# First attention: the first scores of two units copied by one ScalarE instruction across two PSUM banks

## The reference, cut to what matters

```python
q, k, q2, k2, v = (proj(Wq), proj(Wk), proj(Wq2), proj(Wk2), proj(Wv))
q, k, q2, k2 = (_apply_rotary(a, cos, sin) for a in (q, k, q2, k2))
scores = jnp.einsum('bqhd,bkhd->bhqk', q, k)
scores2 = jnp.einsum('bqhd,bkhd->bhqk', q2, k2)
pattern = scores / Dh * (scores2 / Dh)
pattern = jnp.where(causal[None, None, :, :], pattern, 0.0)
z = jnp.einsum('bhqk,bkhd->bhqd', pattern, v)
```

## Time and profile before

| | |
|---|---|
| median of three runs | 1599.43 us |
| lowest and highest | 1596.18 and 1599.50 us |
| the profiled execution, its own time | 1599.61 us |
| its span, first to last instruction | 1597.8 us |
| first attention within the span | about 27 to 575 us |
| copies of first scores, L376 | 384, mean 596 ns |
| products, L443 | 384, mean 686 ns |
| masks, L319 | 256, mean 1273 ns |
| PE busy, share of the span | 75% |
| mean granted TensorE clock | 0.838 of full speed |

### The profile page before, as it was taken

One profiled execution on the slowest core, in us unless ns is written; L12 is line 12 of the kernel. 1 busy time (PEld: TensorE's weight loads), 2 busy tenths in 40 slices (PEclk: granted clock), 3 DMA queues, 4 the chain that ended last, 5 costly groups with the idle time before them and its releaser, 6 DMA issues. The chain is left out here.

```text
span 1597.8 us, 34549 instructions
## 1 busy us (share of the span) xinstructions
PE 1191.3 (75%) x11004; PEld 800.7 (50%) x11004; DVE 972.9 (61%) x2744; ACT 696.4 (44%) x1450; POOL 773.6 (48%) x744
## 2 busy tenths in 40 slices
PE   1899999999999967477887904549996548878880
PEld 0344444444444446256666703449996426656660
DVE  4566666767666654888874043925555488878302
ACT  0666667676766624322222405545552612222240
POOL 0577777777777720045556720035550014446661
PEclk9999999999999965577887956869996557888795
DMA  5000000000000022012112140000003101111217
GB/s 141 1 1 0 0 0 0 0 0 0 0 0 0 1 60 77 3 27 60 50 43 55 53 118 11 0 10 0 0 0 86 50 14 39 45 42 50 56 52 217
DMA packets 67972, 54.50 MB, mean 34 GB/s; under 512 B 12865, under 2 KB 57281, under 8 KB 67905
## 3 DMA queue, kind: packets, MB, share of 16 engines
q1 hardware_dynamic: 51392, 32.70, 7.5%
q0 software_dynamic: 8192, 16.79, 3.7%
q10 hardware_dynamic: 8320, 4.19, 0.9%
HBM read 32.69 MB, written 20.97 MB: 34 GB/s over the span
## 5 line engine op out<-in xcount | busy, mean ns | idle before, releaser
L319 POOL TENSOR_TENSOR patt_aa<-patt_aa,causal_aa 128x512 f32<-128x512 f32 x256 | 319.1, 1273 | 100.8 <-DVE patt_aa L443 100.8
L443 DVE TENSOR_TENSOR patt_aa<-p_second_aa,first_aa 128x512 f32<-128x512 f32 x384 | 247.5, 686 | 163.1 <-ACT first_aa L376 161.3
L1231 POOL DMA_INDIRECT rows_e<-norm_rows,index_e x128 | 123.6, 966 | 369.5 <-DVE index_e L955 329.5
L376 ACT ACTIVATE first_aa<-p_first_aa 128x512 f32<-128x512 f32 x384 | 208.4, 596 | 146.8 <-PE p_first_aa L534 143.0
L534 PE MATMUL p_first_aa<-q_t_aa,k_t_aa 32*128 32x512 f32 x768 | 217.4, 642 | 30.4 <-ACT first_aa L376 30.4
L534 PE MATMUL p_second_aa<-q_t_aa,k_t_aa 32*128 32x512 f32 x768 | 233.3, 642 | 0.0
L1143 PE MATMUL p_cnt_e<-reach_e,ones_e 128*128 128x240 bf16 x448 | 89.8, 337 | 102.9 <-DVE reach_e L1001 102.8
L1246 POOL DMA_INDIRECT ffn_rows<-yb_e,index_e x128 | 130.6, 1020 | 58.1 <-issue 32.3
L1077 PE MATMUL p_h_e<-rows_t_e,w_e 128*128 128x512 f32 x256 | 148.6, 710 | 0.2
L553 PEld LDWEIGHTS p_z_aa<-patt_aa,v_aa 128*32 128x32 f32 x3072 | 74.9, 109 | 123.9 <-issue 68.2
L1194 ACT ACTIVATE hid_e<-p_h_e,b_e 128x512 f32<-128x512 f32 x128 | 87.9, 688 | 102.6 <-PE p_h_e L1077 102.4
(11 more groups left out here) (229 smaller groups left out, 2278.6 us busy)
## 6 DMA issues: line engine op xcount, KB each, us to landing
norm_rows<-norm_n SPq DMA_DIRECT2D x32, 256.0 KB, 2.3
w_e<-L_ffn_w SPq DMA_DIRECT2D x32, 256.0 KB, 2.8
buf_r<-ffn_rows SPq DMA_DIRECT2D x16, 512.0 KB, 5.7
out<-x ACTq DMA_DIRECT2D x8, 512.0 KB, 8.2
rows_e<-norm_rows,index_e POOLq DMA_INDIRECT x128
ffn_rows<-yb_e,index_e POOLq DMA_INDIRECT x128, 2.3
b_e<-L_ffn_b SPq DMA_DIRECT2D x16, 64.0 KB, 3.7
lanes<-c_lanes SPq DMA_DIRECT2D x1, 256.0 KB, 3.0
```

The source lines that it names most:

```text
L319: pool.tensor_tensor(patt[n % LAG][:, b, :, :], patt[n % LAG][:, b, :, :], causal[:, None, :].broadcast_to([P, 4, P]), ALU.mult).then_inc( ...
L376: act.activation(first[n % 2][:, b, :], p_first[b][:], ACT.Identity).then_inc(first_copied, 1)
L443: dve.tensor_tensor(patt[n % LAG][:, b, :, :].rearrange("p h q -> p (h q)"), p_second[(2 * n + b) % ROOMS][:], first[n % 2][:, b, :], ALU. ...
L1231: pool.indirect_dma_start(rows[lpar][:, j, :], None, norm_rows, bass.IndirectOffsetOnAxis(ap=list_of(l, lpar)[:, j:j + 1], axis=0)).then_i ...
```

## The change

The two PSUM tensors of one bank each become one tensor of two banks, and `copy_first` issues one ACTIVATE of 2 x 512 numbers for the two units of a step in place of two ACTIVATEs of 512. It waits for the first scores of both units, and raises `first_copied` by 2 when the whole is done. The matmuls write the same banks as before, in the same order and with the same waits. The products are as before: they wait for `unit + 1`, a count that is now reached for both units at once.

```diff
-        p_first = [ps(f"p_first{i}", [P, 512]) for i in range(2)]
+        p_first = ps("p_first", [P, 2, 512])
...
                 def copy_first(g, n):
-                    for b in range(2):
-                        unit = 2 * (STEPS * g + n) + b
-                        act.wait_ge(first_done, unit + 1)
-                        if later(g) or n >= 2:
-                            act.wait_ge(patt_done, unit - 3)
-                        act.activation(first[n % 2][:, b, :], p_first[b][:], ACT.Identity).then_inc(first_copied, 1)
+                    unit = 2 * (STEPS * g + n)
+                    act.wait_ge(first_done, unit + 2)
+                    if later(g) or n >= 2:
+                        act.wait_ge(patt_done, unit - 2)
+                    act.activation(first[n % 2][:], p_first[:], ACT.Identity).then_inc(first_copied, 2)
...
-                            out = p_second[(2 * n + b) % ROOMS] if kind else p_first[b]
-                            pe.matmul(out[:], k_t[par][rows, half, keys * P:(keys + 1) * P],
+                            out = p_second[(2 * n + b) % ROOMS][:] if kind else p_first[:, b, :]
+                            pe.matmul(out, k_t[par][rows, half, keys * P:(keys + 1) * P],
```

## The result

The changed kernel takes 1633.59 us (median of 4 runs, 1631.69 to 1633.98) against 1598.38 for the kernel before: 1.022 times as long, with a 95% interval of 1.0202 to 1.0237, or 35 us more. The forecast was 28 us more. The profiled execution has a span of 1632.2 us, 34.4 more than before.

What follows compares the result with a forecast made beforehand. A chain across engines paces the first attention's loop, with the first product a link: 30 turns of 0.90 (27.0), turn 30 0.8, the end 0.4, together 28.2 us on 1599.4, so 1627.6 us; range 1612 to 1643.

Steps and rivals of the forecast that it cites:

- The turn and its three parts: One 16.36 us loop turn of the first attention, cut at copies of steps 1, 3, 5; forecast 0.90 longer, 17.25.
- The copy: Merged ACT copy of 1024 numbers: 1.02 us, bounds 0.98 and 1.19; the first product must wait 0.42 longer.
- Part 1: Copy of step 1 to copy of step 3, 5.37 us: no slack, so it takes the whole 0.42.
- Part 2: Copy of step 3 to copy of step 5, 5.52 us: 0.42 less a slack of 0.36, so 0.06.
- Part 3: Copy of step 5 to the next copy of step 1, 5.46 us: no slack, the whole 0.42.
- The last turn: Turn without projections, its chain near even between old and new link: only 0.4 us, for the last product.
- (a): Second scores' late unit runs faster than counted, or another link gives way: 1612 to 1623 us; chance 0.13.
- (b): All six steps take the 0.42: 2.5 us a turn, 1677; with all above 1643, chance 0.07.
- (d): No change: slack unseen in the timelines takes up the 0.42 in parts 1 and 3; 1599 us, chance 0.05.
- (c): Faster: the copies' end, not the product, is the link; 0.12 us a turn gained, 1596 us; chance 0.05.

Runs made afterwards that it cites:

- m1: Changed kernel with the merged copy in step 1 only, the other steps with two copies; ratio 1.0096 to the kernel before, +15.7 us.
- m5: Changed kernel with the merged copy in step 5 only, the other steps with two copies; ratio 1.0096 to the kernel before, +14.9 us.
- the pair of kernels with a constant tile: Kernel before and changed kernel, products multiplying by a constant tile without waiting for copies; 1638.03 and 1639.90 us against 1653.02 of the kernel before.
- m3: Changed kernel with the merged copy in step 3 only, the other steps with two copies; ratio 1.0006 to the kernel before, +0.3 us.
- m024: Changed kernel with the merged copy in steps 0, 2 and 4, two copies in the others; ratio 1.0010 to the kernel before, +1.3 us.
- The halves: Kernel before, unit 0's copy and product halved in steps 1 and 5: 1650.06 against 1650.82 us; also with the copy wait last: 1651.07 against 1651.48.
- shape_b: Kernel before with its two copies of 512 numbers written as patterns of 2 x 256; 1651.30 against 1650.82 us, ratio 1.0000.

## Why the prediction was right, and where it was short

The direction, the mechanism and the range held: 1633.6 in 1612 to 1643, and 35 us where 28 were forecast. By its steps:

- **The turn and its three parts.** That the first product is a link in parts 1 and 3, and nearly one in part 2, was right. m1 and m5 show the two, each by itself, and the pair of kernels with a constant tile shows that nearly all of the loss passes through the product.
- **The copy.** 1.02 was taken, 1.025 measured. By the Trainium skill's page "ScalarE: Activation LUTs", section "What ACT_TABLE_LOAD costs", the estimate was 1.04, so the slope of the trace was the better price. The start of the product behind the copy's start was to be 1.05, and 1.14 in step 1; it is 1.05 to 1.06, and 1.15.
- **Part 1.** +0.42 forecast, +0.51 measured. m1, where copy 3 is as before, has +0.43. The rest is the later start of copy 3: behind scores 3 it is 1.34 (303.03 to 304.37), where the spreads on ACT set 1.26.
- **Part 2.** +0.06 forecast, +0.06 measured, but by two errors that cancel. The slack was some 0.1 larger, as m3 shows, and the merged copy at its end starts 0.10 later behind its scores.
- **Part 3.** +0.42 forecast, +0.55 measured; m5 has +0.44 with an unmerged copy at the end. The rest is again the start of the merged copy.
- **The term that was short** is thus one that the sum put at nothing: a merged copy starts 0.10 us later behind its matmuls. The prediction's words "The waits, their number and the products themselves stay as they were" left it out, and they were wrong for ACT's own wait, which now asks for both units (0.04 of the 0.10). 30 turns of 0.2 are 6 of the missing 7 us.
- **The last turn** was counted at 0.4. Its copies go from 591.00 to 603.12 us, 12.12, where it took 11.48 before (556.72 to 568.20): 0.6. That in the steps without projections the product of unit 0 becomes a link, too, is a guess that no run tested.
- **The rivals.** (a), a late unit that runs faster, is out: in scores 2 the first pass of the late unit starts some 0.8 us behind the scores' start, and the list goes on 1.86 behind that start, as 0.81 + 1.05 wants. (b), every step pays, is out by m024, and (d), no change, by the result. (c), the copies' end is the link, needed a copy of 0.60. Its 0.06 do reach scores 4 in m3 (1.07 behind copy 3, where it was 1.14), and part 2 is 0.06 shorter there than before; the later start of copy 3, 0.08 in part 1, takes it back.

The Trainium skill's rule against the change, in "Perfetto Trace Analysis", section "Optimizing Scalar/DVE Operations", says that breaking up instructions may let work be completed sooner where Scalar or Vector are not saturated but cause bubbles on other engines. This result agrees with it in the one direction that was changed, grouping on an engine busy for 335 of 500 us, which cost 35 us. The halves show its limit: broken up further, the same copy won nothing.

## What to carry to other kernels

Ask of a merged instruction not what it saves on its own engine but who waits for its first half. Here ScalarE saved 12 us of busy time and the kernel lost 35, since VectorE got the first half 0.42 us later in each step and two of six steps in a turn had no slack for it. To find them, sum the chain from one fixed point of the loop to the next: a part whose sum closes to 0.01 has no slack, and a part that is short by 0.36 has at least that. Such a sum prices a delay. It does not price a gain: for that, sum the next chain as well, which in part 1 was only 0.11 shorter.

## What the runs showed of the hardware that was not expected

- One ACTIVATE over two PSUM banks costs nothing for the second bank: 1025 ns for 2 x 512 numbers, 1024 from one bank read twice. Against two of 596 ns that overlap (1.08 us for both) it saves 0.06.
- It starts later behind its matmuls, by 0.05 us with one instruction of 1024 numbers (from one bank too; the same 512 numbers in two rows of 256 do not start later) and by 0.04 with the wait for the second unit, though the two matmuls run side by side. Why was not found.
- The order of three waits ahead of an instruction is not free: with the one that comes last in time also last in the program, the products of steps 2 to 5 started 0.10 us later behind their copies (0.73 against 0.63 from the copy's start), that of step 1 no later (0.70 against 0.72). Why was not tried.
- The same program took 1599 us on one chip and 1651 to 1653 on three others. A turn of the first attention is alike to 0.01 us on both kinds (16.36 in the kernel before and in shape_b), so the difference lies outside that loop; what makes it is open.
